# Two graph layers on one core: gathers of single values held to TensorE's row blocks, and the pairs' chain in another order

## The reference

```python
# layer 0: attention over an adjacency matrix, with scores for listed pairs
q = (x[sub] @ Wq.T + bq).reshape(-1, 8, 64)
k = (x[obj] @ Wk.T + bk).reshape(-1, 8, 64)
att = ((q * k).sum(-1) / np.sqrt(64)).T
scores = zeros((8, n, n)).at[:, sub, obj].set(att)
scores = where(adj == 0, -inf, scores)
scores = scores.at[:, di, di].set(1e-07)
x = layernorm(x + softmax(scores, axis=2).sum(axis=0) / 8 @ x)
# layer 1: attention with 16 heads over the same adjacency
seq = (x @ W_seq).reshape(N, 16, 32)
scores = leaky_relu(seq . a1 [:, None] + seq . a2 [None, :]) + (1 - adj) * -65500
x = layernorm(x + elu(softmax(scores) seq @ W_out + b_out))
```

## Time and profile before

| | us |
|---|---|
| three timed runs | 430.3, 433.04, 433.5 (median 433.04) |
| the profiled execution | 429.68 |
| its span | 427.9 |
| TensorE busy | 353.2 (83%) |
| VectorE busy | 321.1 (75%) |
| ScalarE busy | 202.1 (47%) |
| GpSimd busy | 186.8 (44%) |

### The profile page before, as it was taken

The page is one execution under the profiler, slowest core; times in us unless marked ns, Lnnn a source line. Parts: engine busy times, 40 slices in busy tenths (PEclk is TensorE's granted clock), DMA queues, the critical chain, the costliest instruction groups (busy, mean ns, idle before and its releaser), DMA issues.

```text
span 427.9 us, 5189 instructions
## 1 busy us (share of the span) xinstructions
PE 353.2 (83%) x1648; PEld 215.2 (50%) x1648; DVE 321.1 (75%) x814; ACT 202.1 (47%) x451; POOL 186.8 (44%) x178
## 2 busy tenths in 40 slices
PE   1799999999960786789999998158988999999990
PEld 1345555554420333338887776046554656665650
DVE  2989999768400686758778776769699999999865
ACT  4966755646310020235555533112244676676783
POOL 6656766565477100000000000776887888884000
PEclk9999999999995699879999999589999999999996
DMA  7999335339950012029111111675666567676014
GB/s 265 384 385 353 147 110 183 104 111 253 230 146 0 15 44 93 1 96 373 52 76 53 51 52 77 179 207 152 176 169 182 158 193 232 177 196 182 25 51 154
DMA packets 34758, 65.11 MB, mean 152 GB/s; under 512 B 15648, under 2 KB 16800, under 8 KB 32672
## 3 DMA queue, kind: packets, MB, share of 16 engines
q1 hardware_dynamic: 25632, 42.45, 29.4%
q0 software_dynamic: 9088, 22.20, 19.1%
HBM read 53.50 MB, written 8.52 MB: 145 GB/s over the span
## 4 chain that ended last, share of the span: by engine, by line
DVE 32%; DMA 23%; PE 19%; POOL 14%; issue 9%; ACT 2%; another core or an unknown queue 0%; DVEq 0%; POOLq 0%; SPq 0%
DMA pr<-in_adj_dram,aidx 21%; PE ps L810 12%; DVE adjT L1940 8%; POOL pr L521 7%; POOL adjT L598 6%; PE ps L628 3%; DVE arenaC L1807 2%; DVE ps L1865 2%; DVE adjT L1805 2%; DVE ps L1858 2%; DVE arenaA L1871 2%; DVE stage L1930 2%; PE ps L799 2%; DMA adjT<-seqtab,eidx 1%; DVE stats L1744 1%
## 5 line engine op out<-in xcount | busy, mean ns | idle before, releaser
L628 PE MATMUL ps<-arenaB,adjT 128*128 128x512 f16 x512 | 121.7, 398 | 1.8 <-DVE arenaB L1284 1.8
L521 POOL DMA_INDIRECT pr<-in_adj_dram,aidx x79 | 82.9, 1049 | 51.0 <-DMA pr<-in_adj_dram,aidx 34.9
L598 POOL DMA_INDIRECT adjT<-seqtab,eidx x64 | 77.2, 1206 | 19.5 <-issue 19.5
L628 PEld LDWEIGHTS ps<-arenaB,adjT 128*128 128x128 f16 x512 | 51.5, 102 | 64.6 <-issue 12.3
L924 PE MATMUL ps<-adjT,stage 128*128 128x264 f32 x256 | 66.7, 407 | 19.6 <-DVE adjT L1940 12.5
L598 POOL DMA_INDIRECT adjT<-seqtab,near x16 | 20.4, 1273 | 123.5 <-DMA seqtab<-arenaA 117.1
L924 PEld LDWEIGHTS ps<-adjT,stage 128*128 128x128 f32 x256 | 48.9, 198 | 41.7 <-DVE ps L1865 20.1
L810 PE MATMUL ps<-stage 128*128 128x272 f32 x256 | 61.5, 394 | 0.2 <-ACT stage L1070 0.2
L837 PE MATMUL ps<-adjT 128*128 128x512 f32 x120 | 54.1, 593 | 1.0 <-issue 1.0
L810 PEld LDWEIGHTS ps<-stage 128*128 128x128 f32 x256 | 47.4, 190 | 9.7 <-ACT stage L1070 0.9
L1940 DVE TENSOR_TENSOR adjT<-adjT 128x1024 f32<-128x1024 f32 (+2 forms) x35 | 47.8, 1370 | 1.9 <-issue 1.2
(11 more groups left out here) (274 smaller groups left out, 499.1 us busy)
## 6 DMA issues: line engine op xcount, KB each, us to landing
stage<-in_adj_dram SPq DMA_DIRECT2D x16, 1024.0 KB
seqtab<-arenaA SPq DMA_DIRECT2D x16, 264.0 KB, 2.0
arenaA<-in_x_dram SPq DMA_DIRECT2D x4, 1024.0 KB, 13.1
out_dram<-arenaC SPq DMA_DIRECT2D x16, 256.0 KB
arenaB<-in_x_dram SPq DMA_DIRECT2D x1, 1536.0 KB, 10.7
pr<-in_adj_dram,aidx POOLq DMA_INDIRECT x79
arenaC<-in_L_gnn_Wq_dram SPq DMA_DIRECT2D x1, 1024.0 KB
arenaC<-in_L_gnn_Wk_dram SPq DMA_DIRECT2D x1, 1024.0 KB
```

The costliest lines, as they stand in the source:

```text
L521: g.indirect_dma_start(out=avals[:, t:t + 1], out_offset=None, in_=adj_flat, in_offset=bass.IndirectOffsetOnAxis(ap=aidx[:, t:t + 1], axis ...
L598: g.indirect_dma_start(out=Grow[:, b % GR, k, :], out_offset=None, in_=seqtab, in_offset=bass.IndirectOffsetOnAxis(ap=source, axis=0)).the ...
L628: ins = t.matmul(bank(4 + b % 2), adjT[:, b, j, :], xsplit[:, w, j, :], start=(j == 0 and w == 0), stop=(j == NB - 1 and w == 1))
```

## The change

1. GpSimd: up to four gathers are under way instead of three (one more semaphore). From gather 16 on, every sixth one also waits until TensorE has finished a block: #16 for block 1, #22 for block 2, and so on to #76 for block 11.
2. TensorE: `pair_list` stands directly behind `pair_offsets`. A new small product, `pair_places`, spreads only the two places of each pair, before q and k are made. The biases of q and k become the first products of their sums in PSUM (`pair_biases`), q and k use other banks, and both transposes, biases and q/k products stand in one run. `pair_rows` spreads eight rows instead of ten, and stands behind four products of block 15. The flags' product (`pe_sum_flags`) moves behind block 15.
3. VectorE: the matches of places (`match_pairs`) stand between the listings of blocks 14 and 15. `attend` loses both bias adds; `weigh_pairs` and `share_pairs` lose some short steps; the laying out of the correction (`correction`, now two instructions with its own semaphore `corr_laid`) goes behind `weigh_rows`; half of `measure` becomes `judge`, behind it. The cast of the flag (`raise_flag`) moves ahead of `sum_rows(0)`.
4. ScalarE copies q out of PSUM, and copies `Up` earlier.
5. On VectorE and ScalarE the body for few pairs stands first; on VectorE the whole rest of the program stands inside it (and once more in the other body).

```diff
-    FLIGHT = 3
+    FLIGHT = 4
+    CALM = 16
+    PACE = 6
...
             for t in range(T):
                 if t >= FLIGHT:
                     pool.wait_ge(c_av[t % FLIGHT], 16 * (t // FLIGHT))
+                if t >= CALM and (t - CALM) % PACE == 0:
+                    pool.wait_ge(ax_made, 2 + (t - CALM) // PACE)
...
+            def pair_biases():
+                pe.wait_ge(c_b, 32)
+                for w in range(2):
+                    t.matmul(bank(2 * w), ones[0:1, :], pair_bias[w][0:1, :], start=True, stop=False)
...
-            def pair_rows():
+            def pair_places():
                 pe.wait_ge(row_evac, 2 * SENT)
-                pe.wait_ge(pair_step.sem, pair_step.after(0, "diag"))
...
+                pe.wait_ge(pair_step.sem, pair_step.after(0, "diag2"))
+                t.matmul(ps[:, 3, 256:256 + 2 * FEWER], ones[:], diag2.rearrange("p r e -> p (r e)"), start=True,
+                         stop=True)
                 pe.wait_ge(ue_made, 1)
                 t.transpose(ps[:, 1, 0:P], Ue[:], ident[:]).then_inc(pair_pe.sem, 1)
...
+            multiply(NB - 2, 0, Q)
+            pair_places()
+            pair_turn()
+            pair_biases()
+            pair_qk()
+            multiply(NB - 2, Q, NB)
             count_rows()
+            multiply(NB - 1, 0, 2)
             pair_rows()
-            multiply(NB - 1, 0, Q)
-            multiply(NB - 1, Q, 2 * Q)
-            pe_sum_flags()
+            multiply(NB - 1, 2, 8)
             pair_sums()
-            multiply(NB - 1, 2 * Q, 3 * Q)
+            multiply(NB - 1, 8, 11)
             pair_scatter()
+            multiply(NB - 1, 11, 13)
...
             def last_rows():
                 all_listed()
+                lone_rows()
                 attend()
-                lone_rows()
+                weigh_pairs()
                 measure()
-                weigh_pairs()
                 share_pairs()
                 weigh_rows()
+                correction()
+                judge()
...
+            with dve.If(count < FEWER + 1):
+                last_rows()
+                rest(True)
+            links[0] = at_count
             with dve.If(FEWER < count):
                 last_rows()
+                raise_flag()
                 many_pairs(count)
-            many_end, links[0] = links[0], both
-            with dve.If(count < FEWER + 1):
-                last_rows()
...
+                rest(False)
```

More of the change, by code:

```diff
@@ L168, in two_layer_graph_attention @@
         xwh = part(scores, NB * 2 * H1, [2, D], F16)
-        diag = part(stage, 2176, [10, FEWER])
+        diag2 = part(scores, 0, [2, FEWER])
+        both = part(scores, 2 * FEWER, [P])
+        dup = part(scores, 4 * FEWER, [FEWER])
+        prior = part(scores, 5 * FEWER, [FEWER])
+        diag = part(stage, 2176, [H0, FEWER])
         prod8 = part(stage, 2176, [H0, FEWER])
-        pmat = part(stage, 3456, [4, P])
         xsplit = part(arenaB, 0, [2, NB, D], F16)
@@ L239, in two_layer_graph_attention @@
         NCH = -(-T // CH)
-        pair_step = Stage(sem("pair_step"), ["tot", "hot8", "cur", "diag", "mx8", "akeep", "vsel"])
-        pair_pe = Stage(sem("pair_pe"), ["off", "list", "turn", "q", "k", "cnt", "rows", "bad", "sums", "scat"])
+        pair_step = Stage(sem("pair_step"), ["tot", "hot8", "cur", "diag2", "diag", "mx8", "akeep", "vsel"])
+        pair_pe = Stage(sem("pair_pe"), ["off", "list", "rows2", "turn", "q", "k", "cnt", "rows", "sums", "scat", "bad"])
         A_dve = Stage(sem("A_dve"), [f"hot{c}" for c in range(NCH)] + ["shift", "so", "idx", "prod", "red", "att",
@@ L716, in _ @@
                     pair_offsets()
-                if b == 14:
-                    pair_qk()
+                    pair_list()
                 multiply(b, 2 * Q, 3 * Q)
@@ L1252, in _ @@
             count = how_many(act)
+            with act.If(count < FEWER + 1):
+                last_rows()
+                act_first_norm(True)
+                act_second_layer()
             with act.If(FEWER < count):
@@ L2034, in _ @@
-            misfit = misfits(dve)
-            both = links[0]
-            with dve.If(misfit < 1):
-                sparse()
-            one_end, links[0], lates[0] = links[0], both, 0
-            with dve.If(0 < misfit):
-                dense()
-                for b in range(NB):
-                    add_elu(b, late)
-                for b in range(NB):
-                    last_norm(b, 1)
-            assert links[0] == one_end
+                rest(False)
 _INS = ['x', 'adj', 'L0_gnn_rel_pair_index', 'L0_gnn_Wq', 'L0_gnn_bq', 'L0_gnn_Wk', 'L0_gnn_bk', 'L1_gnn_W_seq',
```

679 lines of the change are left out of this document (348 added, 331 removed).

## The result

| | before | after |
|---|---|---|
| median of timed runs | 431.67 us (429.94 to 433.5, 4 runs) | 417.17 us (415.19 to 420.48, 4 runs) |
| profiled execution, span | 429.68, 427.9 | 415.19, 413.4 |
| ratio | | 0.9725, 95% interval 0.9671 to 0.978 |

The changed kernel is faster by 14.5 us, in the medians and in the profiled pair, where the prediction had 15. That is not the whole story. On a later chip the same code was only 6.7 us faster (423.91 against 430.59, ratio 0.9842, interval 0.9781 to 0.9904), and a variant that looked better on one chip lost 36 us on another.

A forecast was written before the change was run, and what follows sets the result against it. The prediction took the last gather's landing at 140.3 us and the fixed chain behind it as the bound. Gains of 11 (gathers) and 4 (chain) sum to 15, from 429.7 to 414.7, put at 415; range 405 to 423, about 8 in 10.

The forecast's parts named there:

- term A: Last gather: with four under way and gates, it lands at 129.3 instead of 140.3, a gain of 11 us.
- term B: Chain from the last landing to the next layer's first product: 47.1 us instead of 51.1, a gain of 4 us.
- The walk: Estimate of the gathers' issue times under the gates: #16 at 32.9, #76 at 124, last landing 129.3.
- Latency: Gathers' time to land does not grow with the number under way; they are not served in turn.
- step (3): TensorE's places, transposes, biases and q/k products: k at +23.3, 1.3 later than before, spread rows from +30.0.
- step (4): VectorE's listing, matches and test: 1.0 us at the test, diagonal ready at +25.4, so TensorE's order decides.
- step (5): Behind the spread rows, fewer short steps and later correction work: `correct(0)` at +39.2, a gain of 3.9.
- step (6): New wait of `raise_flag` before `sum_rows(0)`, which starts at +41.4 instead of +39.9; a shorter half-clock wait cancels it.
- Step (2): TensorE's half clock behind the offsets: 11 of 24 products cost 0.43, 13 cost 0.217, done at +12.8.
- Gates kept: Rival: gathers keep to the gates, last landing 121 to 124, no clock drop: gain 24.3, 405.4 us; chance 0.13.
- The chain doesn't shorten: Rival: gathers gain as forecast, the chain's gain is eaten by half clock and flag wait: 418.7 us; chance 0.08.
- Slower: Rival: TensorE's clock stays at half through the chain, costing 26 us against 15: 440.7 us; chance 0.03.

## Why the prediction was right, and where it wasn't

The time came out within 0.5 us of the forecast in the profiled run (415.19 against 414.7), and within the range in the median (417.17, 2.2 above 415). The mechanism of both terms held. That the number was so near is in part luck: term A gave 0.4 more and term B 1.0 more than forecast, and an unforeseen loss of 1.9 took them back.

- **Term A**, 11 us forecast, 11.4 in the profile, 9.8 by the count in the kernel with the new gathers alone. The walk held, forecast and then measured: #16 at 32.9 (32.97), #28 at 53.9 (54.95), #52 at 88 (88.21), #64 at 105 (105.06), #76 at 124 (123.40), last landing 129.3 (128.9). One gate was wrong: #34 was to wait for block 4 at 61.7 and left at 63.15 without a wait. Latency was the right reading; eight under way showed it.
- "A loss is excluded as long as the blocks end where they do" is the weak sentence. The condition was named and not priced. On two chips the blocks did not end there: ScalarE was stopped while gathers went out in quick succession, the gates opened late, and with four under way the count began at 136.3 to 139.3 instead of 129.1. Nothing in the trace of before pointed to it; that three under way hide it by making GpSimd pause (34.9 us) is my reading. The time of 423.91 on the further chip lies just outside 405 to 423.
- **Term B**, 4 us forecast, 5.0 in the profile and 4.8 in the kernel with the chain alone. By steps, behind the landing, measured and then forecast: list +4.6 (+4.6); the 24 products done at +12.5 by the next row (+12.8); step (3), q/k +15.7 to +22.7 (k +23.3 forecast), rows +29.3 (+30.0); step (4), VectorE waits 4.5 us for the rows, so TensorE decides, as forecast; step (5), `correct(0)` +38.5 (+39.2); step (6), forecast 1.5, measured 1.5; first transposition +43.2 (+44.2), next layer +46.2 (+47.1).
- Step (2) hit by luck. It takes over the 5.3 us of half clock, which from the offsets at +1.7 end at +7.0; only some 5 of the 24 products, begun at +4.9, fit in before that, and the step counts 11. The clock stayed at 0.50 until +9.9, in which 11 or 12 fit. The forecast's own sign of being wrong, "a clock of 0.5 past the first 6 us of the chain", so came true, and the sum held because the count of products was wrong the other way.
- Step (4) held in the middle and missed the end. "Ordered the other way it falls through" is true of the test; that the untaken body then lies in front of the program's end, and must be jumped over there, I did not follow through. It is the 2.9 us by which the sentence "what lies behind 191.5 ... moves as a block" fails.
- *Gates kept* did not happen with four under way, and wasn't the best case either: without gates the offsets came 3.6 us earlier, on a chip without stops. Its price of 24.3 us was too high: with landings at 125 and 115 the first product of layer 2 came 21.3 us earlier than in the kernel before and the time fell by 17.2 and 17.9, since the clock dropped all the same and the closing stretch grew. *The chain doesn't shorten* describes the time of the chain-only kernel (1.6 us in the spans) but not its reason. *Slower* by TensorE's clock did not happen: half clock for some 10 us, at a price of 1.8 us. It was slower in another way, where the gates are left out, and that is a mechanism I had not listed.
- Also right: VectorE's wait 17.0 (17), TensorE's idle at the offsets 5.5 (6), VectorE's idle at the test 0.58 (under 1.5).

What stays open is what holds ScalarE and TensorE up. The rows speak against busy DMA engines (nearly empty meanwhile), a named engine's semaphore, and the clock (one product takes 0.59 us, the gap beside it 1.5 to 2.2); they show quick gathers beside it on two of the chips, and pauses of GpSimd as what limits it. Whether it is the delivery of instructions, of semaphores or something of the chip's placement, no run separates. Whether the kernel before has short stops on such a chip too, hidden in its wait of 28.8 us, isn't known.

## What to carry to other kernels

When two branch bodies change places, follow the jump to its new place: the one that is saved in the middle may now be taken as the last act of the program, where nothing hides it. More DMAs in flight remove waits of the issuing engine, and those waits may be what leaves other engines room; a pacing that looks like a pure loss on one chip should be taken out only after a run on another. Size each term by a mark near it (a landing, a first product), not by the total, since a term can be right and be spent again 200 us later.

## What the runs showed of the hardware

- A gather of one value per partition can leave every 1.25 us (0.94 busy and 0.30 between); with eight under way GpSimd never waited for a landing, not even beside the row loads (381 GB/s from 5 to 20 us).
- Issued at that pace, on one of the chips, they came with a near standstill of other engines: TensorE one product per 1.4 to 2.8 us, ScalarE stopped for 40 to 55 us, with almost no DMA traffic. Identical code took 411.6 us on one chip and 466.5 on another, where the kernel before took 428.8 and 430.6.
- A taken jump over a long body cost VectorE 5.5 to 5.7 us of idle time in mid-program, and made the end of the span 2.9 us longer when it came last; not taken, 0.6.
- With 5.5 us of idle time, from 125.1 to 130.6, TensorE's clock stood at 1.2 GHz (0.50) from 128.6 to 138.8; 32 filling products in the two waits kept it at 2.4 GHz, and that was worth 1.8 us. With no wait but the 1.91 us in front of the list it fell too (0.55 from 128.7 to 132.0) in one profile, and stayed at 1.00 in another (the kernel without gates on the chip with stops, 181.7 to 187.0).
